# Two of the four early gate/up products of the shared expert, moved from the attention to the stage behind it

## The reference, cut to what matters

```python
out = attn(q, k, v) @ Wo.T                       # third layer, per batch of 64 queries
...
scores = sigmoid(x @ gate_w.T) + bias            # last layer: 16 experts, the best 4 per token
topk_w, topk_idx = top_k(scores, 4)
out = sum over e of ((silu(x @ Wg[e].T) * (x @ Wu[e].T)) * cw[:, e]) @ Wd[e].T
out = out + silu(x @ Sg.T) * (x @ Su.T) @ Sd.T   # the shared expert: every token
```

## Time and profile before

| what | value |
|---|---|
| runs without profile | 734.27, 731.38, 733.59 us |
| the profiled execution | 735.28 us, of which its span is 733.5 us |
| mean granted TensorE clock | 0.987 of full |
| TensorE busy | 686.8 us, 94% of the span |
| VectorE, ScalarE, GpSimd busy | 46%, 27%, 24% |
| attention ends, place of the last projection | 472 us |
| expert loop runs alone from | about 553 us |

### The profile page before, as it was taken

One profiled execution on the slowest core, in us unless ns is written; L12 is line 12 of the kernel. 1 busy time (PEld: TensorE's weight loads), 2 busy tenths in 40 slices (PEclk: granted clock), 3 DMA queues, 4 the chain that ended last, 5 costly groups with the idle time before them and its releaser, 6 DMA issues.

```text
span 733.5 us, 9514 instructions
## 1 busy us (share of the span) xinstructions
PE 686.8 (94%) x2428; PEld 393.0 (54%) x2429; DVE 340.8 (46%) x831; ACT 199.6 (27%) x562; POOL 175.3 (24%) x226
## 2 busy tenths in 40 slices
PE   6999899989999899999999999996898999999992
PEld 3555344435678777777776565543333444444440
DVE  4898333441013756567575577463123333333321
ACT  4443332324224433324332242221011111111110
POOL 2244210100000000040422405263024332233332
PEclk9999999999999999999999999999999999999997
DMA  9999995021000000010113102037776767866643
GB/s 338 412 420 420 422 422 218 0 107 66 1 1 0 1 1 1 1 58 1 57 46 100 57 1 116 0 130 195 246 234 101 190 103 179 235 118 109 102 57 43
DMA packets 47569, 97.39 MB, mean 133 GB/s; under 512 B 5760, under 2 KB 27008, under 8 KB 45856
## 3 DMA queue, kind: packets, MB, share of 16 engines
q1 hardware_dynamic: 17072, 66.13, 24.0%
q0 software_dynamic: 8816, 18.00, 12.7%
q10 hardware_dynamic: 21648, 12.85, 6.0%
HBM read 42.93 MB, written 54.17 MB: 132 GB/s over the span
## 4 chain that ended last, share of the span: by engine, by line
PE 36%; DMA 4%; issue 3%; DVE 3%; ACT 1%; SPq 1%; POOL 1%; another core or an unknown queue 1%; ACTq 0%; POOLq 0%; DVEq 0%
PE ps L1094 28%; PE ps L1249 4%; DMA out<-rq,sidx 2%; PE ps L1085 2%; DMA kv<-in_experts 1%; PE ps L1237 1%; DVE r L959 1%; PE ps L1221 1%; ACT r L675 1%; SPq L389 1%; POOL slot_rows L530 0%; DVE smx L941 0%; DVE r L957 0%; ACTq L389 0%
## 5 line engine op out<-in xcount | busy, mean ns | idle before, releaser
L1094 PE MATMUL ps<-kv,rq 128*128 x432 | 196.1, 602 | 5.9 <-SPq L459 3.0
L1094 PEld LDWEIGHTS ps<-kv,rq 128*128 128x128 f32 x432 | 79.8, 193 | 95.8 <-issue 95.3
L1094 PE MATMUL ps<-zT,r 128*128 128x256 f32 (+1 forms) x400 | 92.9, 388 | 1.5 <-ACT kv L637 0.9
L1249 PE MATMUL ps<-r 128*128 128x512 f32 x192 | 85.1, 593 | 0.0
L560 POOL DMA_INDIRECT out<-rq,sidx x36 | 56.7, 1574 | 115.8 <-DMA out<-rq,sidx 94.6
L1094 PEld LDWEIGHTS ps<-zT,r 128*128 128x128 f32 x400 | 75.0, 190 | 15.6 <-issue 5.0
L675 ACT ACTIVATE r<-ps,snm 128x128 f32<-128x128 f32 x128 | 45.3, 366 | 105.7 <-DVE snm L943 105.7
L530 POOL DMA_INDIRECT slot_rows<-zrow,sloti x32 | 32.5, 1016 | 115.5 <-DVE sloti L1005 107.9
L491 POOL TENSOR_SCALAR ve<-mv 128x1 f32<-128x1 f32 x32 | 7.3, 228 | 220.6 <-DVE mv L856 220.5
L1249 PEld LDWEIGHTS ps<-r 128*128 128x128 f32 x192 | 35.2, 190 | 38.3 <-issue 38.3
L1033 DVE TENSOR_TENSOR rq<-ps,rq 128x256 f32<-128x256 f32 x36 | 15.2, 423 | 82.9 <-ACT rq L730 79.8
(11 more groups left out here) (163 smaller groups left out, 892.3 us busy)
## 6 DMA issues: line engine op xcount, KB each, us to landing
slot_rows<-rq SPq DMA_DIRECT2D x4, 8192.0 KB, 49.7
kv<-in_experts SPq DMA_DIRECT2D x9, 1536.0 KB, 7.5
rq<-slot_rows ACTq DMA_DIRECT2D x136, 64.0 KB
r<-in_Wq SPq DMA_DIRECT2D x1, 3072.0 KB, 21.4
r<-in_Wo SPq DMA_DIRECT2D x1, 3072.0 KB, 10.4
r<-in_ctx SPq DMA_DIRECT2D x8, 256.0 KB, 8.5
xr<-in_x SPq DMA_DIRECT2D x8, 256.0 KB, 8.4
r<-in_shared SPq DMA_DIRECT2D x1, 1536.0 KB
```

Of the source, the lines that this page charges most:

```text
L1094: mm = pe.matmul(out, lhs(k), rhs(k), start=(k == 0), stop=(k == n - 1))
L1249: mm = pe.matmul(ps[:, 7, :], oT[:, j % 2, m, :], wo[:, m, :], start=(m == 0), stop=(m == NQT - 1))
```

## The change

`EARLY` falls from 4 to 2. In the attention the early product of block 1 leaves iteration 28 and takes the place at iteration 29 that was block 2's; the product that stood before pv 31 goes. Blocks 2 and 3 now follow behind the attention and take Silu straight from PSUM: block 2 between gate 6 and the second half of the last projection, block 3 where block 4 was, block 4 where block 5 was, and the rest are put into the written-out list anew: between `count` and `tables` TensorE had sh_gu 6, sh_t 3, sh_d 2, sh_d 3, sh_gu 7, and now has sh_d 2, sh_gu 5, sh_t 3, sh_d 3, sh_gu 6, sh_t 4, sh_gu 7.

```diff
-EARLY = 4
+EARLY = 2
...
-        BESIDE = {25: (0,), 28: (1,), 29: (2,)}
+        BESIDE = {25: (0,), 29: (1,)}
...
-        prog += [("sh_gu", 3), ("pv", NU - 1), ("ln_t", 3, J - 2), ("op0", J - 1), ("gate", J - 2), ("gate_v", J - 2)]
+        prog += [("pv", NU - 1), ("ln_t", 3, J - 2), ("op0", J - 1), ("gate", J - 2), ("gate_v", J - 2)]
         prog += [("sh_silu", j) for j in range(EARLY)]
-        prog += [("op1", J - 1), ("ln_stat", 3, J - 1), ("place", J - 2), ("sh_t", 0), ("sh_gu", 4), ("ln_z", 3, J - 1),
-                 ("sh_d", 0), ("ln_t", 3, J - 1), ("sh_t", 1), ("sh_d", 1), ("gate", J - 1), ("gate_v", J - 1), ("sh_gu", 5),
-                 ("sh_t", 2), ("place", J - 1), ("count",), ("route", 0), ("sh_gu", 6), ("route", 1), ("sh_t", 3),
-                 ("sh_d", 2), ("sh_d", 3), ("sh_gu", 7), ("tables",), ("sh_t", 4), ("sh_t", 5), ("sh_d", 4),
-                 ("sh_t", 6), ("sh_d", 5), ("sh_t", 7), ("sh_d", 6), ("sh_d", 7)]
+        prog += [("sh_gu", 2), ("op1", J - 1), ("ln_stat", 3, J - 1), ("place", J - 2), ("sh_t", 0), ("sh_gu", 3),
+                 ("ln_z", 3, J - 1), ("sh_d", 0), ("ln_t", 3, J - 1), ("sh_t", 1), ("sh_d", 1), ("gate", J - 1),
+                 ("gate_v", J - 1), ("sh_gu", 4), ("sh_t", 2), ("place", J - 1), ("count",), ("route", 0), ("sh_d", 2),
+                 ("sh_gu", 5), ("route", 1), ("sh_t", 3), ("sh_d", 3), ("sh_gu", 6), ("sh_t", 4), ("sh_gu", 7), ("tables",),
+                 ("sh_d", 4), ("sh_t", 5), ("sh_d", 5), ("sh_t", 6), ("sh_d", 6), ("sh_t", 7), ("sh_d", 7)]
```

## The result

The changed kernel took 740.38 us, the median of four runs from 738.25 to 741.43, against 732.63 us for the four runs of the kernel before in the same comparison: a ratio of 1.010, 95% interval 1.0078 to 1.0121. That is slower by more than the 0.5% that a measurement can tell.

What follows compares the result with a forecast made beforehand. VectorE and ScalarE were taken to bound 420.9 to 436.7 us, then TensorE, then `tab`, row loads and the second expert's weights. +1.87 + 4.7 - 3.7 = +2.9 us on 733.6 gave 736.5 us, range 732.5 to 740.5.

Steps and rivals of the forecast that it cites:

- Part 6: Behind `tab`: second expert's weights move with `tab`, loop starts 18.5 us after it, wait and half-clock product stay; nothing added.
- Part 1: Attention, iteration 28: removing the 3.43 us product saves 0 us and leaves TensorE idle about 1.1, 1.6 and 1.9 us.
- Part 2: Before pv 31: removing the product starts pv 31 1.56 us sooner; the other 1.87 us become TensorE idle time.
- Part 3: Before op1 7: sh_gu 2 placed there adds 3.43 us; less part 2, op1 7 to `count` moves by +1.87 us.
- Part 4: Between `count` and `tables`: more products and waits for ScalarE's copies, 15.4 against 10.70 us, so +4.7 us.
- Part 5: Before `tab`: the 3.74 us gap, read as TensorE completions late during a heavy transfer, goes; -3.7 us.
- The second load is quicker: Rival at the second expert's weights: load takes 7.5 instead of 9.45 us, total +1.0, 734.6 us; chance 0.08.
- The clock: Rival in the attention: opened gaps drop TensorE to half rate, costing 1.7 us at the projection at 439, 738.2 us; chance 0.07.

Runs made afterwards that it cites:

- e4: Changed kernel with the step `tables` one product sooner, between sh_gu 6 and sh_t 4; ratio to the kernel before 1.0039.
- e8: Changed kernel unchanged, timed once more beside the kernel before; ratio 1.0052, medians 739.55 against 736.58 us.
- e3: Changed kernel with only block 2's product before pv 31 computed again for nothing; ratio to the kernel before 1.0052.
- e5: Kernel before with the first expert's weights requested after `tab` instead of before it; ratio to the kernel before 1.0061.
- e9: Kernel before with only the order around `tables` from the changed kernel, a product down right behind `tables`; ratio to the kernel before 0.9995.
- e1: Changed kernel with both removed products (iteration 28, before pv 31) computed again for nothing; ratio to the kernel before 1.0066.
- e2: Changed kernel with only block 1's product at iteration 28 computed again for nothing; ratio to the kernel before 1.0082.
- e7: Kernel before with only the product before pv 31 moved behind the attention; ratio to the kernel before 1.0050, medians 740.62 against 736.58 us.
- e12: Kernel before, second expert's weights requested right behind the first's, GpSimd's last eight scatters of ids held until `tab`; ratio to the kernel before 0.9994.
- e6: Kernel before with the second expert's weights requested right behind the first's, ahead of the row loads; ratio 0.9963, 734.02 against 736.58 us.

## Why the prediction was right in part

The time lay inside the stated range, near its upper end, and partly by luck: in the first profile the clock took 4.6 us that the sum left out, and the way from `tab` to the second tile was 3.2 us shorter than part 6 had it.

- **Part 1** (0 us for the product at iteration 28) held: idles of 1.00, 1.46 and 1.75 us against 1.1, 1.6 and 1.9, and the placement not earlier. Its words "So I take 0 us" left out what those idles can do to the clock: nothing in e4 and e8, 2.9 us in e3.
- **Part 2** (-1.56 us) held to the hundredth: 2.78 us from pv 30 to pv 31, in e8 too. **Part 3** (+3.43) held at 3.5; +1.90 against +1.87 at `count` in e8.
- **Part 4** (+4.7) measured +4.55 in the first profile, and 5.2 in e8 (505.02 - 488.93 is 16.09; before 10.92), where the wait behind `count` was 0.56 us; it was 0.1 in the first. `route 1` ended some 4 us ahead, as said.
- **Part 5** (-3.7) had the outcome right and the mechanism wrong. "I read it as TensorE's completions arriving late while a heavy transfer runs" falls with e5, where no weights moved and the gap was 7.08 us. It falls with e9 too, where the gap was gone while the weights moved. In the changed kernel a product down follows on `tables`, as in e9, and that is enough. The coincidence with 315 GB/s was only that. Nor is the gap's price shown: where it alone was removed the time stayed within 0.5%.
- **Part 6** ("the second expert's weights move with `tab`", second tile after 18.5 us) failed: 15.3 us, and 17.0 in e8. The rows took 5.73 us to issue instead of 6.69, and the weights came in under 7.7 us, so the rival "The second load is quicker" partly came true. The first tile, forecast 10.9 us behind `tab`, came after 11.8; the four products down behind `tables` have three waits of 0.46 us for ScalarE's copies, of which the forecast names none. The wait of 4 us in front of the second tile did not come at all, nor the half-clock product behind it that the forecast kept; in the first profile that gave 1.5 us back.
- **The clock** is the term that was mis-sized. "A half-clock stretch costs what it cost above, 5.12 - 3.43 = 1.7 us, if it meets the projection at 439" was right in size for that place (1.66), but the idle before pv 31, which part 2 itself forecast as 1.87 us, was not looked at. That one cost 3.0 us, so the case was worth 4.6 us in the first profile and not 1.7, and its chance of 0.07 was far too low: a fall near 460 came in 3 of 5 profiles without the product before pv 31. Only the second of the two falls goes with the change. The argument against the case, that gaps of 1.21 and 1.27 us had left the clock at 1.00, rested on one execution; e1, e2, e5, e7 and e12 fell behind the same gap at 437. What the Trainium skill (TensorE: Matmul & The Clock Gate, "HAM oscillation") advises, keeping the array fed, spoke against this change, though the waits that it describes are longer than the gaps here. The traces of after, e2 and e7 agree with the advice (0.57 to 0.63 from 458 to 466 us); those of e4 and e8, with the same gaps, stayed at 1.00.

The sum of +2.9 us agrees with e8's comparison, +3.0 us in the medians, but no single execution shows its terms adding up: in e8's trace the loop was quicker than forecast and the clock fell inside it. In the first comparison +7.75 us were measured. Its profile has 4.6 us of clock, 1.66 of which the kernel before can have too, and 1.3 us from ahead of the change. Why its four runs were slower than e8's seven is not shown: the mean clocks (0.9832 and 0.9837) are alike and don't say where it fell.

## What to carry to other kernels

A product that fills idle time of TensorE in a nearly full stretch can be free to keep and costly to move: price it where it lands, and price every gap it leaves, one by one, at half rate for the work behind it that has no slack. One profile that shows the clock at 1.00 behind a gap proves little; read several executions. When two things reach a loop's start together (here the shared work and the weights), moving one sooner buys nothing; look for what can be asked for sooner at no one's cost, as the second expert's weights in e6, where the gain was small.

## What was unexpected

TensorE fell to half rate in a stretch where it was busy for 62.8 of 70 us, behind idles of 1.3 to 1.8 us, and not in every execution of the same program. In the kernel before it did so behind one idle of 1.2 us (e5 and e12). A finished group of 12 small products was not seen by ScalarE for 3.74 us (7.08 in e5) while GpSimd's scatters of ids were in flight and TensorE went idle behind four transposes; one further product behind it, or no scatters, made it 0.
